# Attention over gathered rows: the group mask made on POOL between the gathers

## The reference, cut to what matters

```python
for i in range(3):
    residual = h_cur @ W_res + b_res if i == 0 else h_cur
    q, k, v = (h_cur @ W[i] + b[i] for W, b in ((Wq, bq), (Wk, bk), (Wv, bv)))
    e = edge_attr @ We[i] + be[i]
    ke = k[src] + e
    alpha = (q[dst] * ke).sum(-1) / sqrt(128)
    w = softmax(alpha) over the edges of one dst
    msg = (v[src] + e) * w
    h_cur = relu(mean over heads of segment_sum(msg, dst) + h_cur @ Ws[i] + bs[i] + residual)
out = concatenate([h, h_cur]) @ W_ctr + b_ctr
```

## Time and profile before

| what | us |
|---|---|
| median of 3 runs | 4366.57 |
| lowest and highest | 4356.75, 4371.01 |
| the profiled execution, its time | 4329.4 |
| its span | 4327.6 |
| mean granted TensorE clock, share of full | 0.916 |
| attention, layer 0 | about 1214 to 1980 of the span |
| attention, layer 1 | about 1997 to 2772 |
| attention, layer 2 | about 2789 to 3535 |

### The profile page before, as it was taken

The page is one execution under the profiler, slowest core; times in us unless marked ns, Lnnn a source line. Parts: engine busy times, 40 slices in busy tenths (PEclk is TensorE's granted clock), DMA queues, the critical chain, the costliest instruction groups (busy, mean ns, idle before and its releaser), DMA issues. The chain is left out here.

```text
span 4327.6 us, 82914 instructions
## 1 busy us (share of the span) xinstructions
PE 3495.6 (81%) x22381; PEld 2067.5 (48%) x22381; DVE 1823.4 (42%) x5369; ACT 1433.0 (33%) x3483; POOL 1862.8 (43%) x1907
## 2 busy tenths in 40 slices
PE   4999999947758888876777777667777769999998
PEld 2666666635534444443444444334443444555564
DVE  4666666647523333332333333323333323344222
ACT  3555555522623333332233323222222223122112
POOL 2555555500256665653566656456666630000000
PEclk8999999979879999998888998878898889999999
DMA  5677775656444554555666666556666645443223
GB/s 139 187 200 199 198 196 167 165 115 204 140 136 137 140 136 131 139 137 136 169 176 172 176 175 179 156 155 167 167 164 168 166 111 176 171 177 118 74 97 125
DMA packets 716528, 675.29 MB, mean 156 GB/s; under 512 B 382359, under 2 KB 542945, under 8 KB 716117
## 3 DMA queue, kind: packets, MB, share of 16 engines
q1 hardware_dynamic: 622598, 466.26, 37.1%
q0 software_dynamic: 77008, 200.24, 17.2%
q10 hardware_dynamic: 16768, 6.91, 0.6%
HBM read 530.84 MB, written 142.28 MB: 156 GB/s over the span
## 5 line engine op out<-in xcount | busy, mean ns | idle before, releaser
L2293 POOL DMA_INDIRECT l_y<-s_lrows,l_src x1344 | 1352.6, 1006 | 964.3 <-issue 352.4
L2373 PE MATMUL ps<-l_y,aw_pT 128*63 128x277 f32 x2700 | 436.8, 467 | 259.9 <-ACT aw_pT L2591 249.1
L3404 PE MATMUL ps<-nl_adj,nl_table 126*128 126x504 bf16 (+1 forms) x3150 | 631.4, 357 | 2.3 <-DVE nl_table L3639 2.3
L998 POOL DMA_INDIRECT em_gs<-s_rows,em_idx x400 | 432.3, 1081 | 325.8 <-DVE em_a L1189 147.9
L2357 PE MATMUL ps<-aw_yT,aw_qt 128*63 128x384 f32 x1800 | 377.2, 529 | 120.0 <-DMA aw_yT<-s_dxT 61.2
L3404 PEld LDWEIGHTS ps<-nl_adj,nl_table 126*128 126x128 bf16 x3150 | 301.8, 96 | 299.0 <-issue 5.3
L2750 DVE COPY aw_axd<-ps 128x252 f32<-128x252 f32 x225 | 94.7, 421 | 796.9 <-remote 409.9
L2330 PE MATMUL ps<-ident,l_y 128*128 128x128 f32 x1800 | 281.5, 292 | 150.9 <-issue 83.1
L2373 PEld LDWEIGHTS ps<-l_y,aw_pT 128*63 128x63 f32 x2700 | 195.7, 154 | 431.9 <-ACT aw_pT L2591 279.6
L2591 ACT ACTIVATE aw_pT<-ps 128x381 f32<-128x381 f32 x225 | 109.9, 488 | 736.8 <-remote 506.0
L2577 ACT ACTIVATE aw_yT<-ps 128x512 f32<-128x512 f32 (+1 forms) x525 | 261.4, 536 | 245.2 <-remote 114.7
(11 more groups left out here) (381 smaller groups left out, 5866.1 us busy)
## 6 DMA issues: line engine op xcount, KB each, us to landing
nl_adj<-s_adj SPq DMA_DIRECT2D x20, 3100.8 KB
aw_yT<-s_dxT SPq DMA_DIRECT2D x150, 384.0 KB
aw_geoS<-s_geoS SPq DMA_DIRECT2D x450, 94.5 KB
nl_adj<-s_adj SPq DMA_DIRECT2D x15, 2325.6 KB
ws_msg<-s_msg SPq DMA_DIRECT2D x75, 384.0 KB, 3.8
s_dxT<-aw_yT SPq DMA_DIRECT2D x75, 384.0 KB
aw_qt<-s_qt SPq DMA_DIRECT2D x225, 126.0 KB
s_msg<-em_msg SPq DMA_DIRECT2D x100, 256.0 KB
```

The costliest lines, as they stand in the source:

```text
L998: pool.indirect_dma_start(out=gs[:, u, j, :], out_offset=None, in_=d["rows0"], in_offset=bass.IndirectOffsetOnAxis(ap=slot[:, u, 2 * j:2 * ...
L2293: pool.indirect_dma_start(out=y[:, u, j, 0:W], out_offset=None, in_=table, in_offset=bass.IndirectOffsetOnAxis(ap=src[:, u, j:j + 1], axis ...
L2373: m = nc.tensor.matmul(k.ps[64 * v:64 * v + HW, SUM, 0:SW], pT[:, SLOT[u], j, 64 * v:64 * v + HW], y[:, u, v * TH + j, 0:SW], start=j == 0 ...
L3404: m = nc.tensor.matmul(k.ps[:, bank(i, p), 0:cols * WN], source[:, p, q, b, :], adj[:, a % 2, 0:cols, b * WN:(b + 1) * WN], start=b == 0 a ...
```

## The change

VectorE makes `sel` only, now three windows ahead (`select(w + 3)`), after waiting until the mask of window w - 2 has been made. `off` is made by POOL in three parts of two tiles: after the second, fourth and sixth gather of window w it makes that part of the mask of window w - 2. The last two windows' masks follow the last gather of the layer. POOL's waits for `scored` and `turned` are removed. TensorE's scores wait for `masked`; in layers 1 and 2 its sums get a wait of their own for the product `DX`, which the wait for `OFF` had covered. To stay within the number of semaphores, the two counters of the query weights' preparation are merged into `mixed` and `mixed_c`, with shifted counts.

```diff
-    ready = steps("ready", ["DX", "SEL", "OFF"], U, NW)
+    ready = steps("ready", ["DX"], U, NW)
+    selected = steps("selected", ["SEL"], U, NW)
+    masked = steps("masked", ["OFF"], U, NW)
...
     def gpsimd(pool):
+        def mask(w, u, j):
+            if j == 0:
+                pool.wait_ge(selected.sem, selected.of(w, "SEL"))
+                pool.sem_inc(hop["pool"], 1)
+            m = nc.gpsimd.tensor_scalar(off[:, u, j:j + 2, :, :], bc(sel[:, u, j:j + 2, :].unsqueeze(2), [128, 2, H, HN]),
+                                        -1.0, None, ALU.add)
+            if j == T - 2:
+                m.then_inc(masked.sem, 1)
+
...
             for j in range(T):
-                if started(w, U) and j == 2:
-                    pool.wait_ge(scored.sem, scored.of(w - 3, "S"))
-                    pool.sem_inc(hop["pool"], 1)
-                if started(w, U) and j == 4:
-                    pool.wait_ge(turned.sem, turned.of(w - 2, "T1"))
-                    pool.sem_inc(hop["pool"], 1)
                 pool.indirect_dma_start(out=y[:, u, j, 0:W], out_offset=None, in_=table,
                                         in_offset=bass.IndirectOffsetOnAxis(ap=src[:, u, j:j + 1], axis=0)
                                         ).then_inc(rows_in[u], 16)
+                if started(w, 2) and j % 2 == 1:
+                    mask(w - 2, (u - 2) % U, j - 1)
...
+        masked.prime(pool)
         for u in range(1 if before is None else 0, U):
             gather(u, u)
         with pool.Fori(1, NW // U) as i:
             for u in range(U):
                 gather(U * i + u, u)
+        for u in (U - 2, U - 1):
+            for j in range(0, T, 2):
+                mask(NW - U + u, u, j)
...
-            pe.wait_ge(ready.sem, ready.of(w, "OFF"))
+            pe.wait_ge(masked.sem, masked.of(w, "OFF"))
...
             pe.wait_ge(agr_ok.sem, agr_ok.of(w - 1, "AG"))
+            if l:
+                pe.wait_ge(ready.sem, ready.of(w, "DX"))
...
-        def mask(w, u):
-            s = ready.sem
+        def select(w, u):
+            if started(w, U):
+                dve.wait_ge(masked.sem, masked.of(w - U, "OFF"))
             nc.vector.tensor_tensor(sel[:, u, :, :], bc(k.iota_wn[:, 0:HN].unsqueeze(1), [128, T, HN]),
                                     bc(k.dl[:, bass.ds(w, 1), :].rearrange("p w t -> p (w t)").unsqueeze(2), [128, T, HN]),
-                                    ALU.is_equal).then_inc(s, 1)
-            dve.wait_ge(s, ready.of(w, "SEL"))
-            nc.vector.tensor_scalar(off[:, u, :, :, :], bc(sel[:, u, :, :].unsqueeze(2), [128, T, H, HN]), -1.0, None,
-                                    ALU.add).then_inc(s, 1)
+                                    ALU.is_equal).then_inc(selected.sem, 1)
...
                 weigh(w + 1, (u + 1) % U, i if u < U - 1 else i + 1)
-                mask(w + 1, (u + 1) % U)
+            if not (isinstance(w, int) and w + 3 >= NW):
+                select(w + 3, (u + 3) % U)
...
         weigh(0, 0, 0)
-        mask(0, 0)
+        for u in range(3):
+            select(u, u)
```

More of the change, by code:

```diff
@@ L2140, in attention_windows @@
         xs = sb("xs", [D, CW])
-        w2_in, query_mixed, query_mixed_c = sem("w2_in"), sem("query_mixed"), sem("query_mixed_c")
+        w2_in = sem("w2_in")
         rows_out, qt_out, qs_out, next_src = sem("rows_out"), sem("qt_out"), sem("qs_out"), sem("next_src")
@@ L2467, in mix_queries @@
                                          start=True, stop=True)
-                m.then_inc(query_mixed, 1)
+                m.then_inc(mixed, 1)
             elif n == 1:
-                pe.wait_ge(query_mixed_c, 2)
+                pe.wait_ge(mixed_c, steps + 2)
                 for h in range(2):
                     m = nc.tensor.matmul(k.ps[:, 6 + h, 0:2 * D + GK], wqT[:, h * D:(h + 1) * D], kb[:, h, :], start=True, stop=True)
-                m.then_inc(query_mixed, 1)
+                m.then_inc(mixed, 1)
             else:
-                pe.wait_ge(query_mixed_c, 4)
+                pe.wait_ge(mixed_c, steps + 4)
                 nc.tensor.matmul(k.ps[:, 6, 0:2 * D + GK], wqT[:, 2 * D:3 * D], kb[:, 2, :], start=True, stop=True)
@@ L2513, in turn @@
                 if queries:
-                    pe.wait_ge(query_mixed_c, 7)
+                    pe.wait_ge(mixed_c, steps + 7)
                 pe.wait_ge(mixed_c, steps)
@@ L2770, in mix_queries @@
         def mix_queries(n):
-            dve.wait_ge(query_mixed, n + 1)
+            dve.wait_ge(mixed, n + 2)
             if n == 0:
-                nc.vector.tensor_copy(wqT[:, :], k.ps[:, 6, 0:H * D]).then_inc(query_mixed_c, 1)
+                nc.vector.tensor_copy(wqT[:, :], k.ps[:, 6, 0:H * D]).then_inc(mixed_c, 1)
                 nc.vector.tensor_copy(kb[:, :, D:2 * D + GK], k.ps[:, 7, 0:H * (D + GK)].rearrange("p (h f) -> p h f", h=H)
-                                      ).then_inc(query_mixed_c, 1)
+                                      ).then_inc(mixed_c, 1)
             elif n == 1:
                 for h in range(2):
-                    nc.vector.tensor_copy(abc[:, h, :], k.ps[:, 6 + h, 0:2 * D + GK]).then_inc(query_mixed_c, 1)
+                    nc.vector.tensor_copy(abc[:, h, :], k.ps[:, 6 + h, 0:2 * D + GK]).then_inc(mixed_c, 1)
             else:
-                nc.vector.tensor_copy(abc[:, 2, :], k.ps[:, 6, 0:2 * D + GK]).then_inc(query_mixed_c, 1)
+                nc.vector.tensor_copy(abc[:, 2, :], k.ps[:, 6, 0:2 * D + GK]).then_inc(mixed_c, 1)
                 bias_of = k.ps[:, 7, 0:3 * H].rearrange("p (h t) -> p h t", t=3)
-                nc.vector.tensor_copy(ab[:, :, 0:2], bias_of[:, :, 0:2]).then_inc(query_mixed_c, 1)
-                nc.vector.tensor_copy(ab[0:GK, :, 2:3], bias_of[0:GK, :, 2:3]).then_inc(query_mixed_c, 1)
+                nc.vector.tensor_copy(ab[:, :, 0:2], bias_of[:, :, 0:2]).then_inc(mixed_c, 1)
+                nc.vector.tensor_copy(ab[0:GK, :, 2:3], bias_of[0:GK, :, 2:3]).then_inc(mixed_c, 1)
         def split_geometry(c):
@@ L2829, in vector @@
             before.scalar_done(dve)
-        for s in (ready, soft, indexed, parts_ok, out_ok) + ((geo_ok,) if queries else (joined_ok,)):
+        for s in (ready, selected, soft, indexed, parts_ok, out_ok) + ((geo_ok,) if queries else (joined_ok,)):
             s.prime(dve)
```

## The result

The changed kernel took 4382.25 us (median of 11 runs; two disturbed ones at 5029.63 and 12104.58 are left out of the ratio), the kernel before 4368.81 beside it: ratio 1.0037, 95% interval 1.0020 to 1.0054. It is slower by 0.37%, where 4304 had been forecast: inside the stated range (4185 to 4480), but not the gain that it foresaw. The profiled execution took 4377.48 us (span 4375.6, clock 0.913), 48 us more than that of before.

The account below looks back on a forecast made before the run. No engine was full; POOL's gathers stood for signals arriving late during back-to-back gathers. Terms -414 + 346 + 42 - 37 = -63 us on the median 4366.6 gave 4304 us, range 4185 to 4480.

Parts of the forecast that it names:

- The reading: Attention layers: TensorE's and transfers' signals get through late during back-to-back POOL gathers; longer runs need more quiet, some 2 us a window.
- Step (a): POOL's waits before the third and fifth gather go, those before the first stay: -414 us, between nothing and 414.
- Step (b): 675 masks moved into POOL's gather stream, 630 of them priced at 0.55 us each (ends 0.40 and 1.19): +346 us.
- no difference: Rival on POOL's masks: each costs 0.66 us, one pause exchanged for another, +7 us, 4374 us; chance 0.12.
- Step (c): Waits that remain for POOL in the windows behind the layer starts: 0.2 us a window over 210 windows, +42 us.
- Step (d): Layer starts: masks break POOL's run of five gathered windows, so the sixth window starts earlier: -37 us.
- Step (e): VectorE loses its 62.3 us subtraction but idles anyway: 0; TensorE's scores waiting for POOL's masks counted in the remaining waits.

Follow-up runs that it names:

- e11: The kernel before without its two waits inside a group (before third and fifth gather), masks on VectorE, chip 4: 4543.78 us, 1.0414 of the kernel before.
- e13: The changed kernel with masks back on VectorE and a one-element POOL operation in place of each, chip 4: 4468.37 us, 1.0322 of the kernel before.
- e9: The changed kernel with masks of window w-1, not w-2, made behind the gathers of w, chip 2: 4136.48 us, 1.0985 of the kernel before.
- b2: The changed kernel, unchanged, timed on chip 11: 4267.90 us, 1.1320 of the kernel before.
- e14: The changed kernel with masks of window w-1, not w-2, made behind the gathers of w, chip 4: 4251.11 us, 0.9820 of the kernel before.

## Why the prediction was wrong

**The reading** (signals are late while POOL gathers back to back, and need a rest to clear) is right for the chip of the first profile, and e11, e13 and the mask runs show it on chip 4, which behaves alike; it goes with the chip and not with the kernel. On three others signals are not late, and on the one of them where the change was timed it costs 13%. No row of one profile could tell that.

**Step (a)**, "the waits before the third and fifth gather go", -414 us, is the step that failed in its reason. Taking the waits out gives nothing where signals are punctual (ratios 0.9983, 0.9980, 1.0001) and costs 173 us where they are late. The stands were not what the waits cost; they were the rest that signals needed, and without them POOL stood longer ahead of the first gather. What made POOL's named waits fall anyway, from 534.6 to 99.6 + 19.5 + 0.2 = 119.3 us, was the masks' rest of 0.75 us: without masks 4544, with masks 4382. With the 24 us that POOL stands ahead of masks the fall is 391 us. It has in it the three long stands at the layer starts (50.6 us), which the sum had under (d), so 340 stand against the 372 of (a) and (c). That the size came near is luck: the gain belongs to (b), which was booked as cost alone.

**Step (b)**, 0.55 us a mask, is the term whose size turned the sign. By the groups its price is 421.8 (masks) + 60.4 (gathers longer, 1408.3 - 1347.9) - 43.5 (gaps, 351.2 to 307.7) + 7.5 (the stand ahead of the first mask) = 446 us, 0.66 each of 675, against +346 for 630 at 0.55. Its parts were all off. The gather ahead of a mask does not lengthen (0.95, not 1.36 us), the one behind does (1.03), the gap behind is 0.17 as taken (0.15), but the mask takes 626 ns, not 290: the earlier trace rows, 128 x 128 from f32, was the wrong neighbour for 126 elements over a repeated input. The 1.36 of the earlier trace rows was misread: in the edge stage 95 of the 99 gathers ahead of a copy lie across a two-input operation of VectorE and take 1.36 us on average, the other four 0.98, so it was not the copy that lengthened them. 0.66 us is the price at which the rival "no difference" put the kernel, at 4374; 4382 was measured. The bounds of 0.40 and 1.19 held it.

**Step (c)** left out the mechanism. TensorE's wait for the mask was named under (e) and priced within 0.2 us a window. It is 322.4 us, and what comes back of it is 131 us where signals are punctual (e9 against b2) and some 2% where they are late (e14 at 0.9820 of before, the changed kernel at 1.0037).

**Step (d)** was right in direction. The sixth window starts 43.9, 46.8 and 48.0 us after the first gather instead of 50.7, 55.3 and 51.0: 18 us saved of 37 (the 42.6 in its working is 42.45 by its terms). Most of the rest is three stands that it had left out: 7.5 us ahead of layer 0's first mask, with no wait that explains it, and 9.2 us in two waits for the first selections of the later layers; the longer masks make some 3 us. The first maxima came 7 to 11 us nearer, not 15.

**Step (e)**, VectorE's relief at 0, held: in the kernel before TensorE's mask products had waited 0.9 us in all for L2724.

The layers' sum closes. First to last gather is 2236.8 us before and 2275.0 after (+38), the way from there to the last maximum +7, the start +5, the tail -2: the 48 us of the two spans.

**The two rules.** By "GPSIMD Engine Reference" (When to use GPSIMD) of the Trainium skill elementwise work belongs on VectorE. The trace agrees by more than I had weighed: 3 x 626 ns on POOL against 277 on VectorE, and 13% of the time on chip 11. By "SBUF — State Buffer" of the Trainium skill (Who interferes with whom) a VectorE operation with two SBUF inputs contends with a GpSimd one that reads SBUF, and the one issued second waits for the first to end. The trace agrees. Here the mask starts inside the product L2728 and ends 0.41 us after the selection L2734 that follows it:
```profile
1261.30 0.94 DVE L2728 TENSOR_TENSOR l_y<-l_y 128x768 f32<-128x768 f32 x1
1261.56 1.29 POOL L2285 TENSOR_SCALAR aw_off<-aw_sel 128x126 bf16<-128x126 bf16 x1
1262.17 0.27 DVE L2734 TENSOR_TENSOR aw_sel<-iota_wn,dl_all 128x126 bf16<-128x126 f32 x1
```
Of the 675 masks the 467 that meet no VectorE operation take 562 ns on average and 575 at most; all 67 that take over 640 ns (the longest 1859) lie across a two-input one. They make 43 of the 446 us, 0.06 of the 0.66 us a mask; the rest of its price is there without them.

Not settled: why signals are late on one chip, and whether the first profile's chip and chip 4 are the same one; times and "remote" waits match.

## What to carry to other kernels

A wait that shows idle time may be what lets other engines' signals through: take it out alone, on more than one chip, before its idle time is counted as gain. Price work that is moved onto a dense queue by the queue's stream and by who now waits for its place in the order (e9 has the same masks, only one window less far behind the gathers, and is 131 us faster). And a kernel tuned against one chip's trace is tuned to that chip: here the version that gains 1.8% on one chip loses 9.9% on another.

## What was not expected of the hardware

- The same kernel takes 3768 to 3774 us on three chips, 4369 in the first set and 4333 and 4371 in two sets on chip 4, with the same gathers (1000 and 1007 ns) and a granted clock of 0.95 and 0.92. The difference goes with waits that a "remote" signal ended: none on the three, 513 of them and 1958 us over all engines from 1200 us on in the first profile of the kernel before (rows of the waits, summed).
- Where signals are late, a rest of POOL of 0.75 us behind every second gather lets most of them through (104.3 and 51.1 us of "remote" waits at the maximum), one of 0.42 us few (359.6).
- A one-element operation on POOL between gathers takes 303 to 347 ns on average and costs its stream 0.23 us; 126 elements take 626 to 657 ns, 378 take 1327. Those that meet no VectorE operation take 237, 562 and 1196 ns.
- POOL's row gathers stretch the same way as its masks: in the kernel before 790 that meet no VectorE operation take 947 ns (958 at most), and all 180 over 1.0 us, up to 2.53 us, lie across a VectorE operation with two inputs.
